# A fused state-space, FFN, mixer and expert kernel: banks of B and C lent twice in a state, FFN products from state three on, the second gating factor on GpSimd, mixers in two parts, the weight fold moved

## The reference

```
x = x + scan(ln(x))     # 16 states per feature, h = exp(delta*A)*h + delta*x*B ; y = sum_n h*C + D*x
x = x + ffn(ln(x))      # Hadamard, x@W_up, x@W_gate (2048 wide), silu(gate)*up, Hadamard, x@W_down
x = x + mixer(ln(x))    # (x@W_in_x)@conv_w, z = x@W_in_z (1024 wide), y*silu(z), @W_out
x = x + moe(ln(x))      # 64 experts, top 8, at most 128 rows each, 192 wide, silu gate
```

## Time and profile before

| what | us |
|---|---|
| median of three runs | 1872.94 |
| profiled execution, its time | 1878.37 |
| its span, first to last instruction | 1876.5 |
| chunk 0 (state 0 to the start of chunk 1) | 256.1 |
| chunk 1 | 269.8 |
| chunk 2 | 269.1 |
| chunk 3 | 242.6 |
| drain, to the last down product of mixer 3 | 316.6 |
| rest: four routing tiles and the experts | 473.9 |

### The profile page before, as it was taken

The page is one execution under the profiler, slowest core; times in us unless marked ns, Lnnn a source line. Parts: engine busy times, 40 slices in busy tenths (PEclk is TensorE's granted clock), DMA queues, the critical chain, the costliest instruction groups (busy, mean ns, idle before and its releaser), DMA issues. The chain is left out here.

```text
span 1876.5 us, 19337 instructions
## 1 busy us (share of the span) xinstructions
PE 1535.4 (82%) x5792; PEld 1045.6 (56%) x5792; DVE 1059.2 (56%) x1576; ACT 589.7 (31%) x1031; POOL 791.7 (42%) x491
## 2 busy tenths in 40 slices
PE   6899855698976998958999789999892399889883
PEld 2344322376755776747788667777671255445441
DVE  3787657876678876788788854545323122222220
ACT  3433522254433343533333331212210122222220
POOL 3356732355643444444354424757314332222222
PEclk9999977799987998979999889999895699999997
DMA  6676552168763775774566448986440599999997
GB/s 188 180 212 197 140 170 87 45 202 288 262 207 106 211 230 166 223 237 135 169 194 187 146 118 255 325 298 194 131 143 1 175 321 324 297 294 310 295 298 146
DMA packets 193536, 380.35 MB, mean 203 GB/s; under 512 B 20994, under 2 KB 95106, under 8 KB 192944
## 3 DMA queue, kind: packets, MB, share of 16 engines
q1 hardware_dynamic: 173424, 339.44, 58.8%
q0 software_dynamic: 20032, 39.92, 8.9%
HBM read 301.65 MB, written 124.35 MB: 227 GB/s over the span
## 5 line engine op out<-in xcount | busy, mean ns | idle before, releaser
L1215 POOL TENSOR_TENSOR y<-y,hc 128x2048 f32<-128x2048 f32 x64 | 293.0, 4578 | 320.5 <-DVE hc L1088 320.3
L1071 DVE TENSOR_TENSOR_SCAN bx<-bank,state,bx 128x512 f32<-128x512 f32 x256 | 312.1, 1266 | 4.7 <-ACT bank L781 3.4
L781 ACT ACTIVATE bank<-dl,an 128x512 f32<-128x512 f32 x256 | 170.5, 683 | 281.0 <-DVE bx L1071 280.9
L498 PE MATMUL bank<-xn2T,ring 128*128 128x512 f32 x576 | 232.7, 404 | 15.2 <-DVE xall L948 8.9
L499 PE MATMUL bank<-xn2T,ring 128*128 128x512 f32 x576 | 227.9, 396 | 0.0
L500 PE MATMUL bank<-xn2T,ring 128*128 128x512 f32 x576 | 227.7, 395 | 0.0
L1221 POOL TENSOR_TENSOR act<-th,act 128x512 fp32r<-128x512 f32 x96 | 123.9, 1292 | 240.9 <-ACT act L705 240.6
L1088 DVE TENSOR_TENSOR hc<-bx,bank 128x2048 f32<-128x2048 f32 x64 | 146.2, 2284 | 60.4 <-PE bank L564 53.3
L1400 PE MATMUL bank<-wgu,xeT 128*128 128x384 f32 x512 | 177.6, 490 | 0.0
L509 PE MATMUL bank<-ring,act 128*128 128x512 f32 x384 | 156.1, 407 | 20.6 <-DVE th L937 20.6
L1062 DVE TENSOR_TENSOR bx<-u,bank 128x2048 f32<-128x2048 f32 x64 | 146.1, 2283 | 34.0 <-PE bank L557 28.8
(11 more groups left out here) (150 smaller groups left out, 2379.5 us busy)
## 6 DMA issues: line engine op xcount, KB each, us to landing
ring<-w_all SPq DMA_DIRECT2D x288, 512.0 KB
wgu<-wgu_in SPq DMA_DIRECT2D x64, 768.0 KB
wde<-wd_in SPq DMA_DIRECT2D x64, 384.0 KB
slots<-empty_in SPq DMA_DIRECT2D x16, 1154.0 KB, 9.0
xe<-slots SPq DMA_DIRECT2D x64, 288.5 KB
w_all<-staged_u SPq DMA_DIRECT2D x64, 256.0 KB, 2.8
w_all<-fst SPq DMA_DIRECT2D x48, 256.0 KB, 3.2
w_all<-staged_d SPq DMA_DIRECT2D x32, 256.0 KB, 3.2
```

Source lines behind the costliest of these rows:

```text
L498: nc.tensor.matmul(b[:, :], w[:, k, 0, :], x[:, 0, k, :], start=(k == 0), stop=False)
L781: nc.scalar.activation(dA[k % 2][:, :], dl[c % 2][:, k, :], ACT.Exp, scale=an[:, k, n:n + 1]).then_inc(S_dA, 1)
L1071: nc.vector.tensor_tensor_scan(bx[:, k, :], dA[k % 2][:, :], bx[:, k, :], state[:, k, n:n + 1], ALU.mult, ALU.add).then_inc(S_sc, 1)
L1215: nc.gpsimd.tensor_tensor(y[c % 2][:, :, :], y[c % 2][:, :, :], hc[:, :, :], ALU.add).then_inc(S_ya, 1)
```

## The change

- **Two loans in a state.** PB and PC can be lent in two slots of a state: slot 0 where the loan was, slot 1 after the quanta of the second place (on VectorE after the fourth scan). yT goes to slot 1 of state 0 and slot 0 of state 1, ffn_T to both slots of state 2, mixer_T to both slots of state 15. The mixer's transposed tokens and the FFN's now use tokT[c % 2], so one buffer serves a chunk for both.
- **Spreading.** FFN quanta stand from (c, 3, 0) to (c, 13, 2), 42 places where there were 37.
- **Mixers in two parts** of four pairs (12 quanta each) for chunks 0 to 2: the first from (c, 0, 0) to (c, 3, 0), the second from (c, 13, 2) to (c, 16, 0). In the drain the order is mixer 2 part one, FFN 3, mixer 2 part two, mixer 3. The norm and the transposes of chunk 3 for its mixer stand at places of mixer 2 part two. Routing tiles 8 to 11 move from DRAIN+52 to DRAIN+76 and after.
- **Gating.** ScalarE copies the up bank times its scale to a new SBUF tile ups (`up_out`). VectorE keeps only (tanh+1)*gate. GpSimd multiplies the two (`gated`) one place after up.
- **Fold.** The pieces stand at (0, 13, 1) and every third place after it, and at (1, 1, 0) and every second place after it; before, one in each state from (0, 12, 1) and (1, 1, 1).

```diff
-HALVES = [(kind, c, part) for c in range(NCH) for kind, part in (("ffn", 0), ("ffn", 1), ("mixer", 0))]
+FFN = [[("ffn", c, part, HALF * part, HALF) for part in range(2)] for c in range(NCH)]
+MIX = [[("mixer", c, part, 4 * part, 4) for part in range(2)] for c in range(NCH - 1)] + [[("mixer", NCH - 1, 0, 0, M1)]]
+HALVES = FFN[0] + [h for c in range(2, NCH + 1) for h in MIX[c - 2][:1] + FFN[c - 1] + MIX[c - 2][1:]] + MIX[NCH - 1]
...
-xnt = sb(A, "xnt", [P, 2, D])
-dtr = xnt[0:R, 0, :]
+dtr = sb(A, "dtr", [R, CH])[:, :]
+ups = sb(A, "ups", [P, 2, CH])
-xn2T = sb(A, "xn2T", [P, 2, KT, CH], f32r)
+tokT = [sb(A, "tokT0", [P, 2, KT, CH], f32r)]
-xT = sb(A, "xT", [P, 2, KT, CH], f32r)
+tokT.append(sb(A, "tokT1", [P, 2, KT, CH], f32r))
...
-half_of = {h: i for i, h in enumerate(HALVES)}
+half_of = {h[:3]: i for i, h in enumerate(HALVES)}
+pairs_of = [h[4] for h in HALVES]
+first_pair = [sum(pairs_of[:h]) for h in range(len(HALVES))]
 quanta = [(h, kind, j) for h in range(len(HALVES))
-          for kind, j in [(w, j) for j in range(HALF) for w in ("gate", "up")] + [("down", j) for j in range(HALF)]]
-PER = 3 * HALF
+          for kind, j in [(w, j) for j in range(pairs_of[h]) for w in ("gate", "up")] + [("down", j) for j in range(pairs_of[h])]]
 quanta_at = {}
-def spread(items, places):
+def spread(halves, places):
+    items = [q for h in halves for q in quanta if q[0] == half_of[h]]
+    n = len(places)
     for i, place in enumerate(places):
-        n = len(places)
         quanta_at.setdefault(place, []).extend(items[i * len(items) // n:(i + 1) * len(items) // n])
 for c in range(1, NCH):
-    first = PER * half_of["ffn", c - 1, 0]
     if c >= 2:
-        spread(quanta[first - PER:first], range(state_at(c, 0, 2), state_at(c, 5, 0)))
-    spread(quanta[first:first + 2 * PER], range(state_at(c, 5, 0), state_at(c, 14, 1)))
-spread(quanta[-4 * PER:-PER], range(DRAIN + 2, DRAIN + 2 + 3 * PER))
-spread(quanta[-PER:], range(DRAIN + 6 + 3 * PER, DRAIN + 6 + 4 * PER))
-END = DRAIN + 6 + 4 * PER
+        spread([("mixer", c - 2, 0)], range(state_at(c, 0, 0), state_at(c, 3, 0)))
+    spread([("ffn", c - 1, 0), ("ffn", c - 1, 1)], range(state_at(c, 3, 0), state_at(c, 13, 2)))
+    if c >= 2:
+        spread([("mixer", c - 2, 1)], range(state_at(c, 13, 2), state_at(c, 16, 0)))
+START = DRAIN + 2
+TURN = START + 5 * 12
+END = TURN + 3 * 12
+spread([("mixer", 2, 0), ("ffn", 3, 0), ("ffn", 3, 1)], range(START, TURN))
+spread([("mixer", 2, 1), ("mixer", 3, 0)], range(TURN, END))
-fold_at = {state_at(0, 12 + m, 1): (0, m) for m in range(KT)} | {state_at(1, 1 + m, 1): (1, m) for m in range(KT)}
+fold_at = {state_at(0, 13, 1) + 3 * m: (0, m) for m in range(KT)} | {state_at(1, 1, 0) + 2 * m: (1, m) for m in range(KT)}
 FOLDS, PLAINS = 2 * KT, 2 * M1
 plain_at = {state_at(1, 5, 1) + 3 * i // 2: i for i in range(PLAINS)}
...
-            bank_of[c, 1 + t // 2] = ("yT", c - 1, t)
-            bank_of[c, 3 + t // 2] = ("ffn_T", c - 1, t)
-            if t < 2:
-                bank_of[c, 15] = ("mixer_T", c - 1, t)
-        if c >= 2 and t >= 2:
-            bank_of[c, 0] = ("mixer_T", c - 2, t)
+            bank_of[c, t // 2, 1 - t // 2] = ("yT", c - 1, t)
+            bank_of[c, 2, t // 2] = ("ffn_T", c - 1, t)
+            bank_of[c, 15, t // 2] = ("mixer_T", c - 1, t)
-            bank_of[c, 5 + t // 2] = ("scan_T", c + 1, t)
-            bank_of[c, 9 + t // 2] = ("dt", c + 1, t)
+            bank_of[c, 5 + t // 2, 0] = ("scan_T", c + 1, t)
+            bank_of[c, 9 + t // 2, 0] = ("dt", c + 1, t)
-        borrowed_c[c, 7] = ("xdbl", c + 1, 0)
-mixer_T_in_drain = {(2, 2): DRAIN, (2, 3): DRAIN + 1, (3, 0): DRAIN + 4 + 3 * PER, (3, 1): DRAIN + 4 + 3 * PER,
-                    (3, 2): DRAIN + 5 + 3 * PER, (3, 3): DRAIN + 5 + 3 * PER}
-route_at = [DRAIN + 12 + 5 * i for i in range(12)] + [END + 1 + 3 * i for i in range(4)]
+        borrowed_c[c, 7, 0] = ("xdbl", c + 1, 0)
+mixer_T_in_drain = {(3, 0): TURN + 8, (3, 1): TURN + 9, (3, 2): TURN + 10, (3, 3): TURN + 11}
+EARLY = 2 * TT
+route_at = [DRAIN + 12 + 5 * i for i in range(EARLY)] + [TURN + 14 + 5 * i for i in range(TT)] + [END + 1 + 3 * i for i in range(TT)]
...
-                    pe.wait_ge(S_gt, i - 1)
+                    pe.wait_ge(S_uc, i - 1)
...
             pe.wait_ge(S_al, i + 1)
             for t in range(TT):
                 if j == 0 and t % 2 == 0:
-                    pe.wait_ge(S_gt, HALF * h + HALF - 1 + t // 2)
+                    pe.wait_ge(S_hg, first_pair[h] + pairs - 1 + t // 2)
+                    pe.wait_ge(S_uc, first_pair[h] + pairs - 1 + t // 2)
...
-        def borrowed(c, n):
+        def borrowed(c, n, slot):
             for b, lent in ((PC, borrowed_c), (PB, borrowed_b)):
-                if (c, n) not in lent:
+                if (c, n, slot) not in lent:
                     continue
-                what, of, i = lent[c, n]
+                what, of, i = lent[c, n, slot]
+                if (c, n, slot - 1) in lent:
+                    pe.wait_ge(*returned(*lent[c, n, slot - 1]))
...
         def mixer_T(c, t):
-            if c == 2:
-                pe.wait_ge(S_cm, NS * NCH)
-            else:
-                pe.wait_ge(S_r, RS * 3 * TT)
+            pe.wait_ge(S_r, RS * EARLY)
...
         def tanh(h, j):
-            i = HALF * h + j
+            i, m = first_pair[h] + j, tile_of(h, j)
             act.wait_ge(S_g, i + 1)
             wait(act, S_al, i - 1)
-            m = tile_of(h, j)
             nc.scalar.activation(th[:, i % 2, :], PF[2 * (j % 2)][:, :], ACT.Tanh, scale=gsh[:, m:m + 1]).then_inc(S_th, 1)
+        def up_out(h, j):
+            i, m = first_pair[h] + j, tile_of(h, j)
+            act.wait_ge(S_up, i + 1)
+            wait(act, S_gt, i - 1)
+            nc.scalar.activation(ups[:, i % 2, :], PF[2 * (j % 2) + 1][:, :], ACT.Copy, scale=cs[:, m:m + 1]).then_inc(S_uc, 1)
         def gated_hi(h, j):
-            i = HALF * h + j
-            act.wait_ge(S_gt, i + 1)
+            act.wait_ge(S_gt, first_pair[h] + j + 1)
+            i = first_pair[h] + j
             nc.scalar.activation(act8[:, 0, j, :], th[:, i % 2, :], ACT.Copy).then_inc(S_ah, 1)
...
             for h, kind, j in quanta_at.get(pos - 1, ()):
                 if kind == "gate":
                     tanh(h, j)
+                elif kind == "up":
+                    up_out(h, j)
...
             if c >= 1:
-                if (n, m) in ((2, 3), (3, 2)):
-                    for t in ((0, 1) if n == 2 else (2, 3)):
-                        wait(act, n2.tp, TT * (c - 1) + t - 1 if n == 3 else 0)
-                        normed(n2, c - 1, t, xnt[:, t % 2, :])
-                if (n, m) == (14, 3):
+                if (n, m) == (1, 3):
+                    for t in range(TT):
+                        normed(n2, c - 1, t, spr[:, t, :])
+                if (n, m) == (14, 1):
                     for t in range(TT):
...
                                     dst[:, 0, :, tok].bitcast(fp32), ALU.subtract).then_inc(n.lo, 1)
-        def gated(h, j):
-            i, m = HALF * h + j, tile_of(h, j)
-            g, up = PF[2 * (j % 2)], PF[2 * (j % 2) + 1]
+        def half_gated(h, j):
+            i = first_pair[h] + j
             dve.wait_ge(S_th, i + 1)
-            nc.vector.scalar_tensor_tensor(out=th[:, i % 2, :], in0=th[:, i % 2, :], scalar=1.0, in1=g[:, :],
+            nc.vector.scalar_tensor_tensor(out=th[:, i % 2, :], in0=th[:, i % 2, :], scalar=1.0, in1=PF[2 * (j % 2)][:, :],
                                            op0=ALU.add, op1=ALU.mult).then_inc(S_hg, 1)
-            dve.wait_ge(S_up, i + 1)
-            dve.wait_ge(S_hg, i + 1)
-            nc.vector.scalar_tensor_tensor(out=th[:, i % 2, :], in0=up[:, :], scalar=cs[:, m:m + 1],
-                                           in1=th[:, i % 2, :], op0=ALU.mult, op1=ALU.mult).then_inc(S_gt, 1)
         def down_added(h):
...
-                if kind == "up":
-                    gated(h, j)
-                elif (kind, j) == ("down", HALF - 1):
+                if kind == "gate":
+                    half_gated(h, j)
+                elif (kind, j) == ("down", pairs_of[h] - 1):
...
                 scan(1)
-                borrowed(c, n)
+                borrowed(c, n, 0)
                 side(state_at(c, n, 1))
                 norms(c, n, 1)
                 scan(2)
                 scan(3)
+                borrowed(c, n, 1)
                 side(state_at(c, n, 2))
...
             nc.gpsimd.tensor_tensor(y[c % 2][:, :, :], y[c % 2][:, :, :], hc[:, :, :], ALU.add).then_inc(S_ya, 1)
+        def gated(h, j):
+            i = first_pair[h] + j
+            pool.wait_ge(S_uc, i + 1)
+            pool.wait_ge(S_hg, i + 1)
+            nc.gpsimd.tensor_tensor(th[:, i % 2, :], th[:, i % 2, :], ups[:, i % 2, :], ALU.mult).then_inc(S_gt, 1)
         def gated_lo(h, j):
-            i = HALF * h + j
-            pool.wait_ge(S_const, 1)
+            i = first_pair[h] + j
+            pool.wait_ge(S_gt, i + 1)
```

(7 more changed lines are left out.)

120 lines of the change are left out of this document (62 added, 58 removed).

## The result

| | before | after |
|---|---|---|
| median of four runs | 1869.68 | 1849.38 (1842.08 to 1850.33) |
| ratio | | 0.9883, 95% interval 0.9841 to 0.9925 |
| span of the profiled execution | 1876.5 | 1847.1 |
| chunk 1 starts | 304.5 | 288.4 |
| chunk 1, 2, 3 | 269.8, 269.1, 242.6 | 271.0, 256.0, 229.2 |

The account below looks back on a forecast made before the run. TensorE bounds chunk middles; scan, loans and waits pace the ends. Terms -16 -11 -26 -24 +6 +15 -3 -10 +5 +1 = -63 give 1815 for the profiled execution, 5.4 above the median, so 1810 us; 8-in-10 range 1768 to 1850.

Parts of the forecast that it names:

- the tail: End of the drain: scatters of routing tile 11 now stand against the first of the last four, +1 us.
- Fold, -16: Chunk 0: fold pieces from state 13 run nearly without a gap, state 15 ends at 288.5 instead of 304.5.
- Chunk 1, 2, 3 without gating, -77 with the fold: Chunks: new loans and spreading shorten chunk 1 by 11, chunk 2 by 26, chunk 3 by 24 us; fold 16.
- the rival of the loans: Chunks 2 and 3: states 0 to 2 stay 16.4 us each, same in state 15; about 1825, chance 0.05.
- Mixers in two parts: Mixers: three more turns from up to down, two us each for VectorE adds and a TensorE wait, +6.
- the start of the drain: Drain start: the two last mixer_T are gone, so the first quantum can follow at once, -3 us.
- The turn to mixer 3: Before mixer 3 in the drain: mixer 2 part two covers the norm, -10 us; no TensorE gap over 2.
- Gating in the chunks, +15: Middles of chunks: GpSimd's product queues behind the add where up is last in a state; 5 us a chunk.
- GpSimd in the drain, +5: Drain: GpSimd has 17.3 of 16.5 us a route, for 7 routes; at least 6 delay without slack, 5 taken.
- The ratio of 2 between GpSimd and VectorE: Gating product: VectorE about twice as fast; 96 x (1.29 - 0.75) = 52 us if paid on the path, 1867.
- GpSimd's pace: Rival: GpSimd paces chunk middles at 163, 168, 178 us, 45 instead of the 15; 1840, chance 0.19.
- The ring of 18.2 us a state: Chunk middles: GpSimd's product gates hc in a ring of waits; gain gone at 17.2 a state; slower, chance 0.06.

Follow-up runs that it names:

- vec_all: Changed kernel with both gating operations back on VectorE at up's place, without ScalarE's copy, in all products: 1794.12 us, ratio 0.9592.
- vec_split: Changed kernel with both gating operations on VectorE, (tanh+1)*gate one place after gate, the product one place after up: 1815.82 us, ratio 0.9657.
- vec_drain: Changed kernel with the whole gating on VectorE in the drain only; GpSimd keeps the product in the chunks: 1817.5 us, ratio 0.9736.
- late_half: Changed kernel with only VectorE's (tanh+1)*gate moved from gate's place to up's; GpSimd keeps its product: 1818.16 us, ratio 0.9648.
- late_mix: Changed kernel with (tanh+1)*gate at up's place everywhere and the product on VectorE in the drain alone: 1803.84 us, ratio 0.9591.
- vec_tanh: Changed kernel with the whole gating on VectorE at up's place, and ScalarE's tanh ahead of its rounding copy: 1796.55 us, ratio 0.9555.
- gate_late: Kernel before with only the new gating (ScalarE copy, GpSimd product), but (tanh+1)*gate at up's place: 1898.17 us, ratio 1.0174.

## Why the prediction was wrong

The direction was right, the size was not: -29.4 in the spans for -63. What missed, 34 us, lies in four places: the scan ends 17 late, the drain is 9 longer than the 310.6 of my sum, the tail 3, and the expert stage, which I held still, 5 (within its own spread, see the last section).

- **Fold, -16: right.** 288.4 against 288.5, and alone 17.2. One TensorE piece after another runs from winx's landing on.
- **Chunk 1, 2, 3 without gating, -77 with the fold: nearly right.** vec_all ends the scan at A = 1023.9, where before minus 77 would be 1013.5, or 1017.5 with the 4 for the mixers' turns in the chunks. That is 6 to 10 short. Its middles take 474 us in sum where mine took 464 (142.3 for 135.5 in chunk 3). States 0 to 2 are right in sum only: 48.5, 46.2 and 49.1 for 54, 44 and 44. In after they take 44.8 and 46.5 in chunks 2 and 3, where the rival of the loans had 49.2; the loans did get shorter, so that rival is out.
- **Mixers in two parts, the start of the drain, the turn to mixer 3: too small together.** B - A of vec_all is 294.8, 16.8 less than before, where +2 for the one extra turn in the drain, -3 and -10 make 11. The 6 more offset what the chunks fell short by, so that the near-exact total of vec_all is partly luck. TensorE has no gap over 2 us before mixer 3, as forecast.
- **Gating in the chunks, +15: the step that failed first.** The runs show 25. I priced a state with the up at its last place and let TensorE's slack even out half of it. What I passed over is that the change also moves (tanh+1)*gate forward, from up's place to gate's. There VectorE, which is to begin the next scan, waits for a tanh that ScalarE makes behind the rounding of the pair before. That alone costs 14 us with the product on VectorE (vec_split). I took the product for the suspect; at the late place it costs 1 us in sum, 5.8 in chunk 1 less 6.0 that it wins in chunk 3.
- **GpSimd in the drain, +5: mis-sized by a factor of three to four.** Its term said "at least 6 of delay without slack, and 12", and I took less than either. 20.5 us were measured for the whole new gating (vec_drain), 14.1 for product and copy at the late place (late_half, late_mix). The 17.3 a round is not what the list carried: 13.8 of work in rounds of 19.2. So a list that is full in every round is not the mechanism. What the runs show is that TensorE waits 20.5 us for the row buffer, which the scatters release, and 6.0 to 6.5 when the list has less in it. The steps from the product to that wait stay open.
- **The ratio of 2 between GpSimd and VectorE.** The rule that I weighed from the Trainium skill (GPSIMD Engine Reference, section 4.1, Engine selection) would have put two-input work on VectorE. I priced the move by it at 52 us and wrote 1867, which sets the 52 on top of the 20 already in the sum; in their place it is 1847 for an execution like the profiled one, which took 1848.98. The rule's advice was right for the kernel as changed, and its price of the move came nearer than mine: 45.6 were measured up to B. Where the cost falls is another matter. At 0.54 a pair the 64 pairs of the chunks would cost 35 us and the 32 of the drain 17. At the late place the runs have 1 and 14. The chunks' cost was mostly one of place.
- **The rivals.** GpSimd's pace (1840, 0.19) was nearest in number and in its sign in the drain. Its middles add up to 509 and the measured ones to 506, but this is luck: it had 178, 168 and 163, and they are 191, 171 and 144. "TensorE alone" at 1770 does not hold even without the gating's move: vec_all has 1794, and its middles of chunks 1 and 2 take 174.2 and 157.6, with the stalls that this rival saw thinned. The ring of 18.2 us a state was seen in single states and is not the rule: the middles take 16.1 a state on the mean, and state 10 of chunk 1, the longest at 27.0, takes 23.0 without the product.

## What to carry to other kernels

When an operation of an in-order engine is cut in two, look where each half now stands before pricing the engine that takes the second half: a half that is moved forward to "as soon as its input can be there" makes the engine wait for the slowest chain that leads to that input. Work given to an engine isn't priced by the ratio of two durations, and a count of one full round isn't the mean of all rounds: read busy time and waits over the whole stretch. Look at the chunks one by one too, since a sum near zero can be a cost and a gain. And swap one place before dropping an idea: here one word in one list gave back, in sum, all that the chunks had lost. The best kernels (vec_all, 1794.12, 4.1% under before, and vec_tanh, which the ratios don't tell from it) are the change without its gating.

## What the runs showed that was not expected

- VectorE's 128x512 product with both inputs in SBUF takes 0.69 us at the median and up to 4.79 beside GpSimd's add; (tanh+1)*gate, with an input in PSUM, keeps a mean of 0.67 to 0.69.
- The expert stage, from its first matmul to the end of the span, takes between 380.5 (vec_tanh) and 408.1 us (gate_late) in the profiles, with equal work; before has 396.8, after 402.0, vec_all 394.8. TensorE's wait for the loads of the slots makes most of the difference: 39.1 us in vec_tanh, 66.8 in gate_late. So a difference between two single spans says little about the stage that was edited while it is under some 28 us. Marks inside the trace do: vec_tanh's span (1791.7) is shorter than vec_all's (1794.6) though its last down product ends 10.5 later.
- Early and late place of one 0.69 us operation: 24 us over three chunks with GpSimd's product, 14 without.
- GpSimd's product at the late place: 5.8 us lost in chunk 1, 6.0 won in chunk 3.
